# New order tables for the five engine queues of a Mamba-style layer with a ternary feed-forward, fp32 in, one core

## What is computed

```python
x = L0_attn_u                                         # (8, 1024, 256)
# part 1, the state-space block on _layernorm(x)
zxbcdt = u @ W_in.T
z0, x0 = zxbcdt[..., :512], zxbcdt[..., 512:1024]
dt = softplus(zxbcdt[..., -8:] + dt_bias);  A = -exp(A_log)
xBC = silu(causal_conv4(xBC) + conv_b)                # 512 x, 16 B, 16 C channels
h = exp(dt*A)*h + dt*x_t*B_t;  y_t = h.C_t + D*x_t    # scan over tokens, 8 heads
y = layernorm(y)*ln_gamma + ln_beta
y = sigmoid(y @ W_gate.T + b_gate) * y
x = x + concat([silu(z0)*x0, y]) @ W_out.T
# part 2, the feed-forward on _layernorm(x)
h = gelu(u @ absmean(W_fc).T);  h = layernorm(h)*ln_w + ln_b
x = x + h @ absmean(W_proj).T                         # absmean: weights to -1, 0, 1
```

## Time and profile before

| | |
|---|---|
| median of 3 runs | 1175.05 us |
| the profiled execution | 1172.75 us, of it a span of 1170.7 us from first to last instruction |
| mean granted TensorE clock | 0.983 |
| TensorE busy | 1110.9 us (95%) |
| VectorE busy | 982.3 us (84%) |
| ScalarE busy | 964.5 us (82%), of it 162.9 us in 127 table loads |
| GpSimd busy | 385.6 us (33%) |

### The profile page before, as it was taken

One profiled execution on the slowest core, in us unless ns is written; L12 is line 12 of the kernel. 1 busy time (PEld: TensorE's weight loads), 2 busy tenths in 40 slices (PEclk: granted clock), 3 DMA queues, 4 the chain that ended last, 5 costly groups with the idle time before them and its releaser, 6 DMA issues. The chain is left out here.

```text
span 1170.7 us, 23338 instructions
## 1 busy us (share of the span) xinstructions
PE 1110.9 (95%) x8534; PEld 723.4 (62%) x8534; DVE 982.3 (84%) x1958; ACT 964.5 (82%) x1684; POOL 385.6 (33%) x500
## 2 busy tenths in 40 slices
PE   3888999999999999999999999999999999999996
PEld 1464757566665766766576665757666575757663
DVE  5999999989779998888989897799988897776644
ACT  5969489997798988889878988888889987977855
POOL 1213323425423324242432334334333322424331
PEclk9879999999999999999999999999999999999998
DMA  7421113242424315343323424343352221415454
GB/s 226 132 47 36 30 19 84 54 104 43 91 65 83 75 36 104 69 92 73 73 65 70 87 55 90 83 69 91 60 109 53 58 64 38 93 27 91 90 109 108
DMA packets 238977, 89.14 MB, mean 76 GB/s; under 512 B 207760, under 2 KB 235152, under 8 KB 238864
## 3 DMA queue, kind: packets, MB, share of 16 engines
q1 hardware_dynamic: 238864, 87.67, 35.1%
HBM read 24.32 MB, written 8.39 MB: 28 GB/s over the span
## 5 line engine op out<-in xcount | busy, mean ns | idle before, releaser
L359 PE MATMUL bank<-xnT,win 128*128 128x512 f16 (+1 forms) x1248 | 297.5, 385 | 21.5 <-DMA xnT<-hb 17.7
L359 PEld LDWEIGHTS bank<-xnT,win 128*128 128x128 f16 (+1 forms) x1248 | 122.1, 101 | 155.1 <-issue 28.2
L945 DVE SCALAR_TENSOR_TENSOR cv<-bank,cws,cv 128x510 f32<-128x510 f32 (+5 forms) x240 | 177.6, 744 | 12.4 <-ACT tail L676 3.5
L359 PE MATMUL bank<-yhl,wg 128*128 128x512 f16 x768 | 171.6, 379 | 1.2 <-DVE yhl L1092 1.0
L180 ACT ACT_TABLE_LOAD x127 | 162.9, 1283 | 2.2
L1212 POOL TENSOR_TENSOR cat<-sz,cat 128x512 f16<-128x512 f32 x64 | 82.9, 1298 | 242.9 <-ACT cat L782 242.9
L1208 POOL TENSOR_TENSOR caty<-tg,caty 128x512 f16<-128x512 f32 x64 | 86.2, 1356 | 159.8 <-ACT caty L770 159.8
L587 PE MATMUL bank<-wpj,hT 128*128 128x256 f16 x1024 | 123.3, 276 | 9.2 <-DMA hT<-hb 9.2
L359 PEld LDWEIGHTS bank<-yhl,wg 128*128 128x128 f16 x768 | 73.7, 98 | 91.1 <-issue 3.6
L575 PE MATMUL bank<-wfc,x3T 128*128 128x512 f16 x512 | 124.8, 383 | 2.3 <-DMA x3T<-hb 2.3
L587 PEld LDWEIGHTS bank<-wpj,hT 128*128 128x128 f16 x1024 | 100.1, 99 | 30.2 <-issue 8.4
(11 more groups left out here) (146 smaller groups left out, 2088.1 us busy)
## 6 DMA issues: line engine op xcount, KB each, us to landing
x<-in_x SPq DMA_DIRECT2D x32, 512.0 KB, 4.2
out_y<-x SPq DMA_DIRECT2D x15, 512.0 KB, 3.2
crep<-cv SPq DMA_DIRECT2D x128, 32.0 KB, 2.0
hT<-hb SPq DMA_TRANSPOSE x128, 3.2
caty<-in_wg SPq DMA_DIRECT2D x1, 1024.0 KB, 7.8
x<-in_wout SPq DMA_DIRECT2D x1, 1024.0 KB, 10.3
hT<-in_wfc SPq DMA_DIRECT2D x1, 1024.0 KB, 6.5
hn<-in_wpj SPq DMA_DIRECT2D x1, 1024.0 KB, 10.0
```

Of the source, the lines that this page charges most:

```text
L359: m = eng.matmul(b, lhs(p, k), rhs(q, k), start=(n == 0), stop=(n == len(seq) - 1))
L945: op = eng.scalar_tensor_tensor(cs[0:w, j, 3 - k:T], b[0:w, 0:T - 3 + k], cws[0:w, j, k:k + 1], cs[0:w, j, 3 - k:T], ALU.mult, ALU.add)
```

## The change

Only the five order tables differ. Each holds the same words as before in another order, and TensorE's steps take other banks. No step's code, no wait and no tile is changed. Two lines of the diff, as an example (the tables are 105 such lines):

```diff
 POOL_ORDER = (
-    "a0 a1 l0 l0 H1 a2 l0 c1 c1 c1 c1 c1 y0 y0 y0 y0 a3 l0 k0 k0 k0 H3 k0 y1 y1 y1 y1 l1 l1 c3 c3 a4 k1 k1 c3 c3 "
+    "a0 a1 l0 H1 a2 c1 l0 l0 c1 c1 c1 c1 y0 y0 y0 y0 a3 l0 k0 k0 k0 k0 H3 c3 y1 y1 y1 y1 l1 l1 V0 a4 k1 c3 c3 c3 "
...
 SP_ORDER = (
-    "K0 h0 h0 K0 W0 W0 h1 h1 W0 W0 60 c0 W0 c1 h2 h2 61 h3 h3 r0 c2 62 X0 X0 h4 h4 c3 r1 j0 63 j0 j0 j0 j0 X1 X1 "
+    "h0 h0 K0 K0 W0 h1 h1 W0 W0 60 W0 c0 W0 c1 h2 h2 61 h3 h3 r0 r1 62 c2 X0 X0 h4 h4 c3 j0 63 j0 j0 j0 j0 c4 X1 "
```

## The result

| | median | range, runs | ratio to the kernel before |
|---|---|---|---|
| kernel before, same chip | 1174.64 us | 1173.78 to 1175.53, 4 | |
| changed kernel | 1162.52 us | 1162.08 to 1163.1, 4 | 0.9897 [0.988, 0.9914] |
| changed kernel, another chip | 1162.72 us | 1161.2 to 1164.15, 4 | 0.9897 [0.9879, 0.9914] |

The change makes the kernel 12.1 us faster.

The account below looks back on a forecast made before the run. VectorE bounds the start to about 125 us, TensorE what follows, transposed operands the end; VectorE loses time to GpSimd. Start -1.0, to 300 us -0.5, middle -3.0, loads and end 0: -4.5 from 1175.05, so 1170.5 us, range 1164 to 1180.

Parts of the forecast that it names:

- What bounds the start: Until about 125 us VectorE was said to be the limit, busy 101.5 of 107.4 us with just three short waits.
- The start term: 17.6 to 125 us: fewer collisions, less the wait for the load of in_wpj, together -1.0 us.
- Collisions at the start, -1.5: 17.6 to 125 us: half of perhaps 3 us of VectorE's collisions with GpSimd gone; bounds -3 and 0.
- The load of in_wpj, +0.5: At the start: issued behind the segR copies, it makes the thresholds wait 0 to 1.6 us, taken as 0.5.
- The second rival: At the start: late in_wpj load delays thresholds and the state updates behind them; 1178.2 us, chance 0.11.
- 125 to 300 us, -0.5: VectorE still near the limit, so collisions now and then reach TensorE: -0.5 us, bounds -1.2 and +1.
- 300 to 1100 us, -3.0: Middle: one TensorE wait of 2.6 us gone, the other 9.4 us dealt anew for -0.4; bounds -14 and +9.
- The named wait: At 1047.71 us TensorE waits 2.62 us for a tanh made late by a collision; counted as gone.
- Table loads, 0: On ScalarE: seven loads fewer, 9.0 us, hidden by VectorE's and TensorE's work; 0 by itself, bounds -3 and 0.
- The end, 0: From 1134 us: the same chain after the last output product in both orders; 0, bounds -1 and +2.
- No change: First rival, whole kernel: subtractions fall on other SBUF operations, the middle deals its 12 us anew; -0.5, 1174.5 us, chance 0.24.

Follow-up runs that it names:

- nc0_before: Kernel before, only the eight wide GpSimd subtractions of block 0 replaced by one memset each: 1169.12 us, ratio 0.996.
- sp_after: Changed kernel with the first eleven steps of SyncE's order as in the kernel before: 1161.57 us, ratio 0.9916.
- nc14_before: Kernel before, only the sixteen wide GpSimd subtractions of blocks 14 and 15 replaced by one memset each: 1168.56 us, ratio 0.9956.
- nc_before: Kernel before, all 128 wide GpSimd subtractions replaced by a memset of the same tile: 1152.95 us, ratio 0.9823.
- tl_after: Changed kernel with extra table loads ahead of each block's first silu of the B half, sixteen meant, ten done: 1173.22 us, ratio 1.0007.

## Why the prediction was right in kind and wrong in size

**What bounds the start.** Right: VectorE, whose waits from 17.6 to 125 us are now (to the earlier trace rows):

```profile
DVE st L915 <- DMA x<-in_x: 2.2, 1, 2.2
DVE ec L1021 <- DMA crep<-cv: 0.2, 1, 0.2
DVE cv L945 <- ACT tail L676: 0.2, 1, 0.2
```

They are as small in all as before, so what changed there is its collisions.

The step that failed is the same in two terms, the pricing of the collisions: at the start by half of two rows, and from 300 us on by the one wait that shows on TensorE. The start term was short by some 3 us, the other by some 5.

**Collisions at the start, -1.5: failed.** Measured, it is 4.3 us (nc0_before), more than my bound of 3. I had priced the collisions by what two VectorE rows lost, 1.9 us, and then took half, since the order fixes behind what a subtraction stands and not when it starts. But between 112 and 122 us VectorE lost 0.95 + 0.97 + 0.96 = 2.9 us in three places, of which I showed two, and all of it reached the end of the stretch: the weight subtraction L852 that starts at 122.18 starts at 119.69 in nc0_before, though VectorE was 0.4 us later there at 110. Halving was wrong too: GpSimd's step starts when ScalarE's high half is done, and that when VectorE's product is, so the orders do fix the time closely. The first gate subtraction, at 112.0 us in the kernel before, starts at 112.0 to 113.2 in its four variants by blocks or in whole.

**The load of in_wpj, +0.5.** The chain was as forecast: issue at 47.39 for my 46.5, thresholds at 57.23 inside my 56.8 to 59.0, in part by luck, since the load took 6.2 us and not 7.8, and what follows it a little longer. But it was TensorE that waited (3.24 us at L366) and not VectorE, and sp_after shows no price. The second rival, slower by this load, is out.

**125 to 300 us, -0.5.** The lead was 6.6 us at block 1 and 4.5 at block 3: a little was given back. Small either way.

**300 to 1100 us, -3.0: failed in size.** The named wait, the one before the carried products of block 15, went as forecast, and the idle time is 8.2 us where I had said 8 to 9. But the last two blocks gave 4.9 us (nc14_before), not 2.6. Its trace has 3.8 of them in one place: the first projection behind this wait starts at 1049.80 instead of 1052.87, although this execution was 0.7 us later until 1045, since the own products in between took 1.97 us for 2.91 as well. And the rest of the middle gave about 4 where I had -0.4. I had argued that what isn't a visible wait is dealt anew. The sum over the blocks refutes that: VectorE passes collisions on, even where TensorE shows no single long wait. The 23.3 us that I had worked out from three lines come near the 21.5 of nc_before, and 23.3 times the share that is gone from these lines, (23.3 - 10) / 23.3 = 0.57, would have made 13 us. Both agreements are partly luck: the three lines still lose about 5 us without the subtractions, while others lost as well, and counted over all of VectorE only 9.1 of 32.6 us are gone. No run shows that such a sum is a price.

**Table loads, 0: not settled.** The reason was too broad: ScalarE's busy share of 82% doesn't hide a load by itself, ten added ones cost 0.9 to 1.3 us each in the mean. Whether the seven that went were worth anything isn't shown. With the subtractions replaced, both orders take the same time though one does seven loads more (1152.95 and 1153.76 us), and in the kernel before, moving steps to save seven cost 9 us; the trace of that kernel shows no gain up to 125 us from the two that it saved there. So either they stood at hidden places, or the new order's other moves cost about what they gave. No run separates these. The Trainium skill, "ScalarE: Activation LUTs", section "What ACT_TABLE_LOAD costs", would have a switch to another set at about 2.66 us. The ten added loads are of the set that is there already, so they don't test it; the loads of the kernel before do. Each of its 127 starts within 0.02 us of the end of the instruction ahead of it, and behind 103 of them ScalarE's next instruction starts within 0.03 us, so the drain that the page adds isn't seen here.

**The end, 0.** The lead of 12.2 us at block 15 was 9.4 at the end of the span, so 2.8 us were given back, a little beyond my bound of +2; TensorE's waits for hT are 11.7 us in all.

**The rivals.** No change fell because the collisions that went were not all replaced by others, and those that came, in lines such as L1021, cost less time. The rule of the Trainium skill in "SBUF — State Buffer", section "Who interferes with whom", that a VectorE instruction with at most one SBUF input, outside the 2-port modes, doesn't contend with GpSimd, agrees with the trace: the three taps beside the two subtractions took 0.77 us each. It had the consequence right that I gave too little weight, that at a good place the loss is gone whole and not halved; but not every subtraction got such a place.

## What to carry to other kernels

Where one engine is nearly saturated, add up what its instructions lose against their own median, line by line, over all lines, and take the sum as a sign of how much is at stake, beside the waits that show on the engine behind it. It is no price: here 32.6 us of lengthening cost 21.5 us of time in one order, and 23.5 cost 8 to 9 in the other. The price is had by taking the neighbour's reads away, stage by stage. Here GpSimd's reads of SBUF and VectorE's products out of SBUF held each other up, and the cure was the neighbour: put the GpSimd operation beside VectorE's PSUM reads. An order that is tuned across five queues is one object: splicing two, or moving four steps for a good local reason, lost more than it won here.

## What the runs showed that I had not expected

- Ten extra table loads of 1.283 us cost 9 to 13 us on an engine that is 82% busy. My theories had counted sixteen. One early load cost about 3 us by itself, another none.
- The granted clock of the stretch from 17.6 to 125 us was 0.90 in the kernel before and in tl_after, 0.97 and 0.94 in two executions of the changed kernel. In tl_after one table load more, at 42.5 us, is all that differs there from the changed kernel up to 60 us. It is one execution each, and the other variants lie between 0.89 and 0.95 whatever their time (nc_before, at 1152.95 us, has 0.92), so the clock is no measure of the gain; what part of the start's lead is its doing stays open.
- Even without the wide subtractions the longest EM product takes 1756 ns. It starts at 403.86 us, while the bias addition, the one wide SBUF operation left on GpSimd, runs from 403.35 to 405.07:

```profile
L1063 DVE SCALAR_TENSOR_TENSOR EM<-EM,Gm x128: 675/684/1756, 53.4 to 1039.1; 128x512 f32<-128x512 f32 x128
```

```profile
L1221 POOL TENSOR_TENSOR x<-x,r 128x512 f32<-128x512 f32 x32 | 43.3, 1374 | 0.0
```
